# The column sums' products moved in front of the run of value products, in an attention and feed-forward kernel

## The reference

```
q, k, v = x wq, x wk, x wv          # per head, 64 wide
scores  = q k^T / sqrt(64)
probs   = softmax(scores, axis=-1)  # exp(s - max) / sum over all 1101 keys
o       = probs v
h       = h + concat(o) head_kernel
h       = h + ffn(layernorm(h))     # gating, shared and routed experts
```

## Time and profile before

| | us |
|---|---|
| median of 3 runs (lowest, highest) | 4614.39 (4612.45, 4618.93) |
| the profiled execution | 4612.8 |
| its span | 4611.0 |
| PE busy | 4430.4 (96%) |
| DVE busy | 3220.9 (70%) |
| POOL busy | 2955.3 (64%) |
| ACT busy | 2297.3 (50%) |

### The profile page before, as it was taken

How to read it: one execution, slowest core, us unless ns; L and a number is a source line. 1 busy time by engine, 2 the same in 40 slices (tenths; PEclk the granted TensorE clock), 3 DMA queues, 4 the chain that set the end, 5 groups by cost and what they waited for, 6 DMA issues and landing times.

```text
span 4611.0 us, 93821 instructions
## 1 busy us (share of the span) xinstructions
PE 4430.4 (96%) x26597; PEld 3346.4 (73%) x26597; DVE 3220.9 (70%) x7726; ACT 2297.3 (50%) x5640; POOL 2955.3 (64%) x1800
## 2 busy tenths in 40 slices
PE   5999999999999999999999999999999999999996
PEld 3667777777777777777777777777777777777775
DVE  5567768577675877768687675776758777686754
ACT  1555545455544545545455454555445455455541
POOL 0776666666666666666666666666666666666661
PEclk7999999999999999999999999999999999999998
DMA  2111111111111111111111111111111111111000
GB/s 54 34 36 40 32 31 41 36 29 33 44 28 38 32 35 39 31 35 39 35 32 33 34 38 38 28 32 43 28 38 34 33 39 33 33 39 38 23 23 19
DMA packets 157318, 159.02 MB, mean 34 GB/s; under 512 B 66960, under 2 KB 148615, under 8 KB 156807
## 3 DMA queue, kind: packets, MB, share of 16 engines
q1 hardware_dynamic: 156807, 152.68, 13.4%
HBM read 59.63 MB, written 19.65 MB: 17 GB/s over the span
## 4 chain that ended last, share of the span: by engine, by line
PE 88%; DVE 5%; issue 3%; ACT 2%; DMA 1%; POOL 0%; SPq 0%; ACTq 0%; DVEq 0%; POOLq 0%
PE o_ps L796 24%; PE work L689 13%; PE scores L777 13%; PE scores L779 11%; PE work L748 7%; PE work L732 4%; PE work L680 3%; PE work L709 3%; PE work L673 2%; DVE part_max L940 2%; PE work L700 2%; DVE h_out L985 1%; PE work L737 1%; ACT probs L882 1%; PE work L720 1%
## 5 line engine op out<-in xcount | busy, mean ns | idle before, releaser
L1171 POOL TENSOR_TENSOR sums<-sums,probs 128x736 f32<-128x736 f32 (+3 forms) x1344 | 2376.5, 1768 | 700.2 <-ACT probs L882 627.5
L882 ACT ACTIVATE probs<-scores 128x368 f32<-128x368 f32 (+3 forms) x3456 | 1460.2, 475 | 1692.1 <-PE scores L779 1645.8
L940 DVE TENSOR_REDUCE part_max<-work 128x1 f32<-128x368 f32 (+3 forms) x3456 | 1634.3, 530 | 379.2 <-PE work L689 367.9
L777 PE MATMUL scores<-q_a,k_a 128*128 128x368 f32 (+3 forms) x3456 | 1201.6, 348 | 82.4 <-issue 57.4
L796 PE MATMUL o_ps<-probs,values 128*64 128x368 f32 (+1 forms) x6912 | 1161.2, 480 | 0.0
L779 PE MATMUL scores<-q_b,k_b 128*128 128x368 f32 (+3 forms) x3456 | 1150.4, 333 | 0.0
L689 PE MATMUL work<-k_a,q_a 128*128 128x368 f32 (+3 forms) x3456 | 923.3, 352 | 9.4 <-DMA k_a<-k_a 4.9
L796 PEld LDWEIGHTS o_ps<-probs,values 128*64 128x64 f32 (+1 forms) x6912 | 468.1, 138 | 539.5 <-issue 472.8
L777 PEld LDWEIGHTS scores<-q_a,k_a 128*128 128x128 f32 (+1 forms) x3456 | 639.7, 185 | 241.3 <-issue 132.9
L689 PEld LDWEIGHTS work<-k_a,q_a 128*128 128x128 f32 (+1 forms) x3456 | 589.9, 185 | 175.0 <-issue 136.3
L779 PEld LDWEIGHTS scores<-q_b,k_b 128*128 128x128 f32 (+1 forms) x3456 | 643.2, 186 | 14.4 <-issue 4.2
(11 more groups left out here) (183 smaller groups left out, 4370.6 us busy)
## 6 DMA issues: line engine op xcount, KB each, us to landing
sums<-inverse_rows SPq DMA_DIRECT2D x192, 184.0 KB
k_a<-k_a SPq DMA_DIRECT2D x128, 184.0 KB, 2.7
q_b<-q_a SPq DMA_DIRECT2D x128, 184.0 KB, 4.7
k_a<-k_a SPq DMA_DIRECT2D x64, 183.0 KB, 2.7
q_b<-q_a SPq DMA_DIRECT2D x64, 183.0 KB, 6.8
resid_rows<-heads_t SPq DMA_DIRECT2D x16, 576.0 KB, 4.3
h_out<-resid_rows SPq DMA_DIRECT2D x16, 576.0 KB, 8.3
heads_t<-in_pe_table_dram SPq DMA_DIRECT2D x16, 512.0 KB
```

Of the source, the lines that this page charges most:

```text
L777: nc.tensor.matmul(o, k_a[p % 2][i][:, t * P:t * P + n], q_a[p % 2][i][:, c0:c0 + cw], start=True, stop=False)
L882: nc.scalar.activation(probs[0:n, slot(s), i, 0:cw], scores[0:n, h % SB, 0:cw], ACT.Exp, scale=DH ** -0.5).then_inc(probs_ready, 1)
L940: nc.vector.tensor_reduce(part_max[0:n, i * IMG + j if j < IMG else 2 * IMG + i, c:c + 1], w[0:n, 0:keys], AX.X, ALU.max).then_inc(drained ...
L1171: nc.gpsimd.tensor_tensor(acc, acc, probs[0:n, slot(s), :, 0:cw], ALU.add).then_inc(sums_done, 1)
```

## The change

Eleven of the twelve `s` letters of the table move, and INVERT goes from 2 to 1.

```
-INVERT, SCALE_LAST = 2, 8
+INVERT, SCALE_LAST = 1, 8
...
-|pmmm/mpmmmm/p/mpmsm/mmm/|/mmm/mmmm/mmmm/
+|pmmm/mpmmmm/p/mpmm/mmm/s|/mmm/mmmm/mmmm/
...
-m|mm/mmmmu/mmm/msm/mm/r|///
+m|mm/mmmmu/mmm/mm/mm/rs|///
```

More of the change, by code:

```diff
@@ L87 @@
 k/|/k/skmmk/pkmm/pmk|/pmmm/pm/mmpmm/
-|pmmm/mpmmmm/p/mpmsm/mmm/|/mmm/mmmm/mmmm/
[L89 to L97, removed]
-m|mm/mmmmu/mmm/msm/mm/r|///
+|pmmm/mpmmmm/p/mpmm/mmm/s|/mmm/mmmm/mmmm/
+tmm|mm/mtmmm/mmtmm/mmmm/g/rs|vv/vv/vv/k/
+u|c/vk/kuu/ukm/kmums|/mmkum/u/mmm/mum|um/
+mmmum/mmm/um/mmm/mmm/s|mmmumm/mmm/mmu/ummm/
+|mmm/mmmum/mmmu/mmm/muu/s|m/vrvuu/uu/uu/
+|uk/ku/uuk/mkm/mkkm/s|x/mmem/e/mmm/
+|/mmmum/mmmmu/mm/mmm/mmummm/s|mmmmm/mfm/mfuummm/
+|mfm/mmm/mmm/mmm/mmmu/ms|r/uv/vvuvuv/vvvuv/
+k|/kuu/uku/kmm/kmm/s|ku/mmu/mmmm/umm/
+|mmm/mmmuu/mmmm//mmmmm/ms|mmum/umm/mmm/mummm/
+m|mm/mmmmu/mmm/mm/mm/rs|///
 """.split("/")
```

## The result

The changed kernel takes 4662.25 us (median of 4 runs, 4660.89 to 4671.18) against 4613.42 before (4 runs, 4611.29 to 4618.93): ratio 1.0108, 95% interval 1.0091 to 1.0126. It is 49 us slower. The forecast was 4620 with a range of 4588 to 4645, so the time lies outside it, on the side the forecast leaned to, but 42 us off. The profiled execution took 4660.9, its span 4659.1, 48.1 longer than before.

A forecast was written before the change was run, and what follows sets the result against it. PE, 96% busy, was taken to bound the kernel, with DVE holding it in stretches. Stretches before the runs +21, loop's end -13, epilogue -1, inverses 0: +7 us on 4612.8, so 4620, range 4588 to 4645.

The forecast's parts named there:

- The failed step: Inverses' way to POOL: broadcasts 1 to 3 us later, made up by POOL within the chunk; 0, upper bound +20 us.
- Rival D: Inverses to POOL: POOL's scale starts 1 to 3 us later, ACT waits for a buffer of probabilities; 4652 us, chance .07.
- DVE reaches the end of that step ... later than the small load lands: DVE's reciprocal one step behind the sum: it doesn't wait for the sum's load and adds nothing.
- The sum's own price: A sum in front of the run of value products: .45 us of PE time each, against .64 in its old place.
- Rival B: Between sum and run: no drain between the two widths, .14 less 176 times, 25 us; 4595 us, chance .20.
- What the stretches give back: Eleven stretches before the runs: PE gains only where DVE lets it; net 1.4 us per batch, +21 in all.
- Rival C: Stretches before the runs: PE bound by itself, each moved sum gives .19 us; 4567 us, chance .10.
- The loop's end: PE's idle time at 13 branches falls to 3.45 us each as item 10's broadcast leaves later: -13 us.
- rival A: Batch's end: gives nothing back, idle time at the loop's ends stays at 4.4 us; 4633 us, chance .25.

The follow-up runs named there:

- Experiment 3: The kernel before, every sum in its old place, only item 0's reciprocal, store and broadcast one step later: 4647.0 us, 1.0074 of before.
- experiment 12: The changed kernel, all products in place, with item 0's reciprocal in its sum's step instead of one behind: 4635.1 us, 1.0042 of before.
- experiment 8: Against experiment 1: in step 23 sum 1 stands ahead of the turned maxima, in PE's order and in SP's: 4636.0 us, 1.0048 of before.
- experiment 1: The changed kernel with sum 0 alone back in step 12, its reciprocal still one step behind: 4648.6 us, 1.0074 of before.
- experiment 5: The kernel before, with SP issuing item 10's broadcast only once PE has done the batch's last scores: 4594.1 us, .9958 of before.
- experiment 6: The kernel of experiment 5, but item 10's broadcast and the residual's load wait for the next batch's first scores: 4680.6 us, 1.0144 of before.

## Why the prediction was wrong

**The failed step** is the one on the inverses: "So I price it at 0, with +20 (about the present wait once more) as upper bound", which rested on "ACT waits for POOL only 16.7 us" and on DVE, "so it doesn't wait". POOL's lateness did not reach ACT through POOL's buffers, so that row stayed at 16. It reached ACT through DVE. Experiment 3 puts 33 us on item 0's lateness in the kernel before, experiment 12 27 us in the changed one. Rival D had the lateness right, and the way wrong, and its .07 left it out of the range. The trace of before had shown it: L1031 at 1.43 us for 9 columns beside L1032 at .16. I had priced each engine's slack by the waits between engines, and a wait inside an instruction has no row there.

**"DVE reaches the end of that step ... later than the small load lands"** was wrong for two of twelve: item 10, where it costs nothing, since DVE has nothing else (4.5 us of waiting at the end of a batch), and item 1, whose load stands behind the rows of maxima. I had counted what stands behind the moved load in SP's queue, not what stands behind the store that waits for the reciprocal. What the load's place costs in the changed kernel isn't shown: experiment 8 against experiment 1 gained 13 us, of which 5 stand at a step that it explains.

**The sum's own price** was right: .45 a piece, .26 of entry, the same with the width of 64 columns behind it. Rival B (.31) is out by the rows of sums 9 and 10. The Trainium skill's rule in TensorEngine Tiling (Array Packing), Key Properties, agrees with that.

**What the stretches give back** was right in kind (sums 0, 3, 4, 5, 9 and 10 within .1 us) and too hopeful by .8 us a batch together. Rival C is out. The largest miss among them is sum 2, +.81 for +.45. PE after, batch 5:

```profile
1555.79 0.43 PE L689 MATMUL work<-k_a,q_a 128*128 128x368 f32 x1 [0.33 <-DVE q_a L933]
1556.44 0.52 PE L700 MATMUL work<-sums,ones 128*32 128x184 f32 x8 [0.21 <-DVE part_max L940]
1556.89 3.31 PE L796 MATMUL o_ps<-probs,values 128*64 128x368 f32 x20
```

The sum needs a bank of its own, and waits for DVE to empty it. The run needs none, so before it could start while DVE was behind. A unit put between DVE-bound work and the run makes the run wait for DVE: that term was missing. In step 31 the changed kernel's L700 waits for DVE in 12 batches, 2.3 us in all, and L689 in 10, 3.3 in all; the kernel before has neither wait.

**The loop's end** was right on the gap, and the term was sized at half: -24 us over the 13 ends for -13. The gap shrank as forecast, 4.4 to 3.5 (46 of 57 us left), so rival A is out. As much again came from steps 0 and 1 behind the gap, for which I had counted nothing. The means over the 13 loop ends, with the granted clock of the 7 us that start with the first score behind the gap:

| kernel | broadcast leaves, against PE's idle moment | gap | clock | step 0 | step 1 |
|---|---|---|---|---|---|
| INVERT = 1 alone | -3.37 us | 6.68 us | .62 | 2.31 us | 4.80 us |
| before | -1.04 | 4.42 | .60 | 2.78 | 4.80 |
| experiment 5 | +.24 | 3.38 | .75 | 2.23 | 4.00 |
| changed | +.64 | 3.50 | .69 | 2.31 | 4.30 |
| experiment 6 | +5.21 | 3.38 | .61 | 2.24 | 4.91 |

Step 1 goes with the clock: .5 us shorter at .69 than at .60. The gap doesn't set this clock by itself, since experiments 5 and 6 have the same gap at .75 and .61; what does is open. Step 0 isn't a matter of the clock: with INVERT = 1 alone it is as short as in the changed kernel, at .62. In the kernel before, PE waits behind step 0 for ACT's first exponential at 11 of the ends, 4.0 us in all, and in the changed kernel nowhere. PE before, behind the end of batch 9:

```profile
2857.45 0.67 PE L777 MATMUL scores<-q_a,k_a 128*128 128x368 f32 x1 [0.40 <-ACT probs L882]
```

The Trainium skill's page Runtime: NRT & Kernel Launch, section Instruction fetch mechanics, says that a taken branch whose target isn't at hand forces a fetch of it before the engine goes on; the idle time of 3.4 us at each branch agrees with that, though no row shows the fetch, and the rows add that a transfer begun ahead of it makes it longer.

**In numbers:** +2.4 a batch at sum 1 and +.8 on the other stretches, less .9 at the loop's end, is 2.3 more than forecast, 27 us over batches 2 to 13. The other 14 of the 41 us (48 for a forecast of 7) are in the first two and last two batches: mostly the same rows again, and steps 3 and 4 behind a batch's start (+1.7 in batch 1, +3.4 in batch 15), where PE waits 6.0 us for the copies of k in place of 2.5 and on which I ran nothing.

## What to carry to other kernels

Before an operation that another engine waits for is moved later, look at the durations of that engine's neighbours, not only at the waits: an instruction that takes 1.4 us where its like takes .2 is a wait without a row, and a shift of 1.4 us on GpSimd can bring it onto the path. In a queue that works in order, follow what stands behind the instruction that waits, not only behind the one that moves. A unit that needs a buffer is not free in front of one that needs none.

## What was not expected of the hardware

A VectorE operation of .2 us took up to 1.8 beside GpSimd's additions of 1.8 us and ended within .06 us of them. PE stood 3.4 us on the mean at each branch, which no timing of the two transfers lowered, and 6.7 with a broadcast of 184 KB begun 3.4 us ahead. And in two batches of the changed kernel (8 and 10) the run of step 23 took 5.0 us in place of 3.3, at a granted clock of .53 in the window 2379.4 to 2383.0, though PE had been busy throughout the 3.4 us ahead of it at 1.00; this wasn't followed up.
